# Layer 3's split row maxima and the hidden rows' clip move from VectorE to GpSimd, under a newly searched order table

## The reference, cut to what matters

```python
def _act_quant(x):
    scale = 127.0 / jnp.clip(jnp.max(jnp.abs(x), axis=-1, keepdims=True), 1e-05)
    xq = jnp.clip(jnp.round(x * scale), -128.0, 127.0) / scale
...
    gate = jax.nn.silu(_bitlinear(x, w_gate))      # 256 -> 1024
    up = _bitlinear(x, w_up)
    return _bitlinear(gate * up, w_down)           # 1024 -> 256, its input quantised too
...
    scores = jnp.einsum('bqhd,bkhd->bhqk', qh, kh)  # layer 3
    weights = jax.nn.softmax(scores, axis=-1)
```

## Time and profile before

| | |
|---|---|
| median of 3 runs | 1171.27 us (1168.84 to 1176.38) |
| the profiled execution, own time | 1171.04 us |
| its span in the trace | 1169.3 us |
| PE busy | 1042.6 us (89%) |
| DVE busy | 925.1 us (79%) |
| ACT busy | 805.6 us (69%) |
| POOL busy | 550.9 us (47%) |
| mean granted clock of PE | 0.977 |

### The profile page before, as it was taken

How to read it: one execution, slowest core, us unless ns; L and a number is a source line. 1 busy time by engine, 2 the same in 40 slices (tenths; PEclk the granted TensorE clock), 3 DMA queues, 4 the chain that set the end, 5 groups by cost and what they waited for, 6 DMA issues and landing times.

```text
span 1169.3 us, 26077 instructions
## 1 busy us (share of the span) xinstructions
PE 1042.6 (89%) x8257; PEld 776.2 (66%) x8298; DVE 925.1 (79%) x3387; ACT 805.6 (69%) x1484; POOL 550.9 (47%) x1097
## 2 busy tenths in 40 slices
PE   7989999999999988889888998888898999989986
PEld 6667778776788865766666765545566565656654
DVE  4779987878465678798986589999998999899744
ACT  5667666656665556647575667657889798899963
POOL 7232364655212456467841117756454444434343
PEclk9899999999999998989999999889999999999999
DMA  7984322325768642412358954323122222221000
GB/s 226 325 282 142 91 73 56 91 73 164 202 192 221 186 126 73 131 60 62 102 177 264 271 172 140 102 73 93 44 77 64 82 56 55 83 55 52 14 10 27
DMA packets 102326, 140.02 MB, mean 120 GB/s; under 512 B 12336, under 2 KB 79792, under 8 KB 102192
## 3 DMA queue, kind: packets, MB, share of 16 engines
q1 hardware_dynamic: 98688, 129.57, 37.8%
q0 software_dynamic: 3072, 8.39, 2.3%
q10 hardware_dynamic: 432, 0.39, 0.1%
HBM read 65.43 MB, written 22.54 MB: 75 GB/s over the span
## 4 chain that ended last, share of the span: by engine, by line
PE 39%; DVE 25%; ACT 13%; issue 7%; DMA 7%; SPq 5%; POOL 4%; DVEq 0%; another core or an unknown queue 0%; POOLq 0%; ACTq 0%
PE ps L1545 9%; PE ps L1674 4%; PE ps L1584 4%; PE ps L1566 3%; DVE ps L2239 3%; ACT probs L1996 3%; PE ps L1767 3%; PE ps L1538 3%; DVE ps L2231 3%; SPq L2862 2%; PE ps L1552 2%; DMA w<-in_expert 2%; ACT q_st L2013 2%; DVE bn L2122 2%; DVE neg_max L2243 2%
## 5 line engine op out<-in xcount | busy, mean ns | idle before, releaser
L1996 ACT ACTIVATE probs<-ps 128x384 f32<-128x384 f32 (+1 forms) x512 | 260.3, 545 | 88.8 <-PE ps L1587 52.3
L1566 PE MATMUL ps<-k_st,q_st 96*128 96x256 bf16 (+1 forms) x1024 | 173.0, 266 | 32.9 <-DVE neg_max L2231 11.8
L1584 PE MATMUL ps<-q_st,k_st 104*128 104x256 bf16 (+1 forms) x1024 | 179.5, 264 | 20.8 <-ACT probs L1996 13.0
L2013 ACT ACTIVATE q_st<-ps 8x1024 bf16<-8x1024 f32 x128 | 130.0, 1016 | 33.5 <-PE ps L1655 28.4
L1566 PEld LDWEIGHTS ps<-k_st,q_st 96*128 96x128 bf16 x1024 | 85.5, 100 | 88.9 <-DVE neg_max L2231 21.8
L2231 DVE CUSTOM_DVE_ANT_0 ps<-ps,diag_s 128x128 f32<-128x128 f32 (+1 forms) x384 | 123.4, 358 | 20.9 <-PE ps L1566 19.4
L1584 PEld LDWEIGHTS ps<-q_st,k_st 104*128 104x128 bf16 x1024 | 91.2, 99 | 66.2 <-ACT probs L1996 19.3
L2560 POOL TENSOR_SCALAR var_eps<-mv 128x2 f32<-128x2 f32 (+1 forms) x115 | 29.1, 253 | 209.9 <-DVE mv L2125 205.5
L1674 PE MATMUL ps<-probs,v 128*32 128x256 f32 (+1 forms) x2048 | 125.9, 366 | 1.7 <-ACT probs L1996 0.8
L2239 DVE CUSTOM_DVE_ANT_0 ps<-ps,mask_s 128x256 f32<-128x256 f32 x256 | 101.7, 451 | 6.8 <-PE ps L1566 6.5
L2630 POOL CAST parts<-qf 128x512 bf16<-128x512 f32 x64 | 40.1, 626 | 117.2 <-DVE qf L2152 50.6
(11 more groups left out here) (273 smaller groups left out, 2546.8 us busy)
## 6 DMA issues: line engine op xcount, KB each, us to landing
k_st<-parts SPq DMA_DIRECT2D x192, 128.0 KB
q_st<-parts SPq DMA_DIRECT2D x189, 128.0 KB
w<-in_expert SPq DMA_DIRECT2D x62, 384.0 KB, 4.3
x_rows<-wo SPq DMA_DIRECT2D x10, 768.0 KB, 10.2
ctx_t<-in_ctx_t SPq DMA_DIRECT2D x16, 256.0 KB, 3.0
ring<-x_rows SPq DMA_DIRECT2D x31, 128.0 KB, 3.4
y_rows<-ring SPq DMA_DIRECT2D x31, 128.0 KB, 3.5
xn_t<-x_rows SPq DMA_DIRECT2D x31, 128.0 KB, 4.1
```

The source lines that it names most:

```text
L1566: last = mm(t[:, c0:c0 + n], head(q_st, r, h, KROWS, j * P, P), head(k_st, r, h, KROWS, 0, n), start=j == 0 or not by_pe, stop=not by_pe, ...
L1584: last = mm(t[:, j * S:j * S + n], head(k_st, r, h, KALL, j * P, P), head(q_st, r, h, KALL, skip, n), start=j == 0 or L == 3, stop=L == 3, ...
L1996: nc.scalar.activation(probs[:, (hg % 2) * HPG + h4, 0:width], tile_of(key)[:, 0:width], ACT.Exp, scale=SCALE).then_inc(*tile_drained(key))
L2013: nc.scalar.activation(out, tile_of(key)[KROWS:KALL, 0:S].unsqueeze(1).to_broadcast([2 * HPG, HPG, S]), ACT.Copy).then_inc(*tile_drained(key))
```

## The change

Three things are changed, and the table with them.

In layer 3 (`SPLIT_BY_G = (3,)`) the two split instructions of each of the 32 groups are POOL's, in a step of their own (`split_max`) with a new lane, `max_splits`; `reduce` on DVE ends with the reduction. `turn_max` waits for the new signal `split_made` in layer 3. DVE waits for `split_made` before the first reduction of each group of the item behind a layer 3 item, since that reduction writes where POOL may still read. `hidden_clip` is the same instruction on POOL. `normalise` on DVE gets a wait for its own previous reading of `sum_inv`. Last, all tuples of `AT` are new (a search with random delays in it), and they move steps in all five queues.

```diff
-AT = (
+AT = (
...
+SPLIT_BY_G = (3,)
...
+def max_splits(part):
+    for L, b in ORDER:
+        if L in SPLIT_BY_G:
+            for hg in range(HG):
+                yield
+                part.split_max(L, b, hg)
...
-    lanes += [f(part) for f in (max_turns, max_copies, weighted_values, value_copies, value_turns, value_shares)]
+    lanes += [f(part) for f in (max_splits, max_turns, max_copies, weighted_values, value_copies, value_turns, value_shares)]
...
-                    pe.wait_ge(*max_made.at((L, b, hg)))
+                    pe.wait_ge(*(split_made if L in SPLIT_BY_G else max_made).at((L, b, hg)))
...
+                    if h4 == 0 and SLOT[L, b] and ORDER[SLOT[L, b] - 1][0] in SPLIT_BY_G:
+                        dve.wait_ge(*split_made.at((*ORDER[SLOT[L, b] - 1], hg)))
...
-                    if h4 < HPG - 1:
+                    if h4 < HPG - 1 or L in SPLIT_BY_G:
                         return
...
+                    if pair:
+                        wait_drained(dve, ("ot", L, b, pair - 1))
+                    elif SLOT[L, b]:
+                        wait_drained(dve, ("ot", *ORDER[SLOT[L, b] - 1], HG // 2 - 1))
                     V.reciprocal(sum_inv[:, :, :], t[:, :, :, DH]).then_inc(*inverted.step((L, b, pair)))
...
-                def hidden_clip(T):
-                    dve.wait_ge(*hid_round.at(T))
-                    if T >= SJ:
-                        wait_filled(dve, ("ht", T - SJ))
-                    V.tensor_scalar(hid_q[:, T % SJ, :], hid[T % SJ], ROUND, Q_MAX, ALU.subtract, ALU.min).then_inc(*hid_ready.step(T))
...
+                def split_max(L, b, hg):
+                    if hg > 1:
+                        wait_filled(pool, ("t", L, b, hg - 2))
+                    elif SLOT[L, b]:
+                        wait_filled(pool, ("t", *ORDER[SLOT[L, b] - 1], hg + 2))
+                    wait_drained(pool, ("m", L, b, hg, HPG - 1))
+                    full = neg_max[:, hg, :, :].rearrange("p h j -> p j h")
+                    hi, lo = [max_parts[:, hg % 2, :, KROWS + n * HPG:KROWS + (n + 1) * HPG] for n in range(2)]
+                    G.tensor_copy(hi, full).then_inc(*split_hi.step((L, b, hg)))
+                    pool.wait_ge(*split_hi.at((L, b, hg)))
+                    G.tensor_tensor(lo, full, hi, ALU.subtract).then_inc(*split_made.step((L, b, hg)))
+
+                def hidden_clip(T):
+                    pool.wait_ge(*hid_round.at(T))
+                    if T >= SJ:
+                        wait_filled(pool, ("ht", T - SJ))
+                    G.tensor_scalar(hid_q[:, T % SJ, :], hid[T % SJ], ROUND, Q_MAX, ALU.subtract, ALU.min).then_inc(*hid_ready.step(T))
```

More of the change, by code:

```diff
@@ L1477, in build @@
         max_hi = signal("max_hi")
+        split_made = signal("split_made")
+        split_hi = signal("split_hi")
         own_ready = signal("own_ready")
@@ L1510, in build @@
         class Idle:
-            score = exp = maxima = reduce = turn_max = rows = values = copy_output = output = normalise = k_out = lambda *_: None
+            score = exp = maxima = reduce = split_max = turn_max = rows = values = copy_output = output = normalise = k_out = lambda *_: None
             k_hi = k_rest = k_low = k_stack = q_out = q_hi = q_rest = q_low = q_stack = v_out = v_take = v_copy = ln = ln_power = lambda *_: None
```

## The result

The changed kernel takes 1191.29 us (median of 4 runs, 1181.43 to 1194.22), the kernel before 1172.01 us beside it (4 runs, 1168.84 to 1176.38). The ratio is 1.0147, 95% interval 1.0108 to 1.0185: the change made the kernel 1.5% slower, where 0.7% faster was forecast. In a later job (e14) the ratio of the same two kernels was 1.0178 (1.0133 to 1.0223). PE's mean granted clock is 0.966 in this profiled execution and 0.977 in the one of before; "What stays open" comes back to it.

A forecast was written before the change was run, and what follows sets the result against it. PE sets the pace to 700 us; from 700 to 1050 us DVE is fuller and holds PE up. The middle of -5.3 us (-11.9 + 6.6) and -12.1 us, -8.7 us, gave 1162.5 us, range 1148 to 1178.

The forecast's parts named there:

- What is put on POOL: Step pricing the moved splits and clips on POOL: 31.7 us of work, 6.6 us put back on the path.
- The term of 16 x 1.12 us: POOL's work for the sixteen hidden-row clips, each priced at 1.12 us like L2620.
- The term on the path: PE's waits for the clip in the middle stretch: three at 1.12 us each, 3.4 us.
- DVE's relief of 30.5 us: DVE busy time removed by moving 32 groups' splits (16.7 us) and 16 clips (13.8 us).
- PE's loads were to wait under 15 us for maxima: Expected profile sign, first scores' weight loads from 700 to 1050 us: under 15 us where they waited 24.1.
- The splits' price: Cost of layer 3's two split instructions on POOL: 0.22 + 0.21 us, 0.50 us a pair with the wait between.
- rival (4): At `turn_max` in PE's queue: POOL's in-order queue delivers splits late, +13.7 us, 1185 us; chance 0.12.
- Rival (2): The new table frees PE's idle time in the first 700 us, 10.7 us more, 1152 us; chance 0.13.
- Rival (3): The read port shared by DVE and POOL takes the relief back: -2.3 us, 1169 us; chance 0.15.
- the forecast's -8.7 us: Whole-kernel gain, the middle of a count by the chain (-5.3 us) and one by DVE's queue (12.1 us).
- 12.1 us of the loads' waits for maxima: Count by DVE's queue: half of PE's 24.1 us of weight-load waits for row maxima vanishes.
- the 12.2 steps for 8.5 of the turns: New table's PE steps between a layer 3 group's last `maxima` and its turn, covering a POOL late by two or three.

The follow-up runs named there:

- e14: The changed kernel measured once more, unaltered, against the kernel before in a later job: 1.0178, 1182.00 us beside 1165.14.
- e8: Kernel before plus sixteen POOL instruction forms behind the last store, timed singly: on 1024 values mult with add 1.05 us, subtract with min 3.65.
- e5: Changed kernel with POOL's clip written as mult by 1.0 and add -ROUND, without the limit to 127: 0.9919 of the kernel before, 1162.38 us.
- e1: Changed kernel with layer 3's splits and the clip back on DVE, so only the new table remains: 1.0021 of the kernel before, 1167.05 us.
- e7: Kernel before with its old table, only layer 3's splits moved to POOL: 1.0012 of the kernel before.
- e9: Kernel before with its old table, only the clip moved to POOL, in the mult-and-add form: 0.9994 of the kernel before.
- e10: Kernel before with its old table, layer 3's splits and the mult-and-add clip both on POOL: 1.0066 of the kernel before.
- e15: Changed kernel with the mult-and-add clip on POOL, measured again in a later job: 0.9933 of the kernel before, 1156.76 us beside 1165.14.
- e2: Changed kernel with only the clip back on DVE; layer 3's splits stay on POOL, new table: 0.9961 of the kernel before, 1159.03 us.
- e6: Changed kernel with POOL's clip as a single subtraction of ROUND, no second operation: 1.0019 of the kernel before.
- e16: Changed kernel with the clip on DVE and six useless subtract-with-min instructions at its POOL place, not waiting for DVE's clip: 1.0163 of the kernel before.

## Why the prediction was wrong

**The step that failed** is in "What is put on POOL": "The clip has the length and kind of L2620: 1.12 us." It has the length, not the kind. L2620 multiplies and adds; the clip subtracts and takes a minimum, and that is 3.65 us on POOL (e8). The term of 16 x 1.12 us was 16 x 3.7 us. The term on the path fell with it: three waits of 1.12 us, 3.4 us, were seven waits and 14.6 us in the same stretch, and 34.6 us of clips on the chain; in e5, with the short clip, PE's waits for it are 0.8 us. No bound was drawn for the clip's length, which was the second fault: a price was taken from the nearest row by size, as if the operations made no difference.

The trace of before did hold a warning, in rows that the prediction doesn't use. These are POOL's instructions of the routing; L2706 is add with mult, L2741 mult alone, both on 16 elements, and L2743 add with max on 32:

```profile
L2706 POOL TENSOR_SCALAR nblk<-cnt x8: 202/203/203, 149.9 to 572.0; 128x16 f32<-128x16 f32 x8
...
L2741 POOL TENSOR_SCALAR less<-nblk x8: 269/274/281, 154.7 to 576.8; 128x16 f32<-128x16 f32 x8
...
L2743 POOL TENSOR_SCALAR past<-past x8: 327/333/337, 155.4 to 577.5; 128x32 f32<-128x32 f32 x8
```

One operation takes 71 ns more than two on the same 16 elements. And if 0.2 us of L2743 are the start, some 0.1 us remain for 32 elements, over 3 ns each, which scaled to 1024 would have given 3 to 4 us instead of 1.12.

**The other terms.** DVE's relief of 30.5 us was 34.8 by the busy times, or 27.2 against the new table with the old work (e1). PE's loads were to wait under 15 us for maxima in the middle stretch and waited 18.6. The splits' price was right, and the place of rival (4) was not the trouble: PE waited for POOL's splits once in the changed kernel, for 0.7 us. Its mechanism, an in-order queue on POOL that comes late, has a part in the loss all the same, behind the clip: three of the ten pieces on the chain, 8.4 us. Rival (2) fell with e1: the table alone is 1.0021, and the first 700 us were unchanged. Rival (3), the port: with a clip of about the assumed length the change does pay, so the port doesn't take the whole relief back. The Trainium skill's warning (page "Perfetto Trace Analysis", section "Optimizing Scalar/DVE Operations") that offloading between these two might not help holds for e7, e9 and e10 in its outcome, and not for e5 and e15.

**The sum with the right clip.** Where the clip takes the 1.12 us of the forecast, as in e5 and e15, the kernel stands at 0.9919 and 0.9933 of before; the forecast's -8.7 us of 1171.04 are 0.9926. So the sum was close with that term in the place of the other. That it was close for its reasons is not shown, and may be luck. The sum let 12.1 us of the loads' waits for maxima vanish. From 620 us to the end these waits are 28.0 us before and 21.8 in e5, 6 us less. In e10, with the same moves under the old table, they are 22.4, and the kernel is at 1.0066: the relief alone doesn't give the gain.

**By the length of the clip,** splits on POOL and the new table throughout:

| the clip | mean us of one | ratio |
|---|---|---|
| on DVE (e2) | 0.75 | 0.9961 |
| on POOL, mult and add (e5, e15) | 1.12 | 0.9919, 0.9933 |
| on POOL, subtract (e6) | 2.86 | 1.0019 |
| on POOL, subtract and min (changed, e14) | 3.70 | 1.0147, 1.0178 |

From 1.12 to 3.70 us are 2.58 x 16 = 41 us on POOL, and they cost (0.0147 - (-0.0081)) x 1172 = 27 us by the first pair, which is from two jobs, and 1182.00 - 1156.76 = 25 us by e14 and e15, side by side in one. So somewhat under two thirds of it came through.

**What stays open.** How the slow clip's loss divides between late rows and a held queue isn't measured: the case of late rows with a free queue wasn't tried. The chain of the changed kernel gives the larger part to the late rows, 26.2 us against 8.4, and e16 shows only that a somewhat longer hold is enough by itself.

A part of the loss shows as PE's own busy time. With the same 8298 matmuls on record, PE is busy for 1048.9 us at a mean granted clock of 0.974 in e14 and 1038.5 us at 0.984 in e15, 10 of the 25 us between the two, and all of it behind 620 us. Whether the lower clock only follows from PE's longer waits isn't shown; the two kernels differ in nothing but the clip's form, so it is brought about by that form in one way or another.

Nor is it settled why the moves pay under the new table and not under the old one (old: splits 1.0012, clip 0.9994, both 1.0066; new, from 1.0021: splits 0.9961, clip 1.0001, both 0.9919 and 0.9933). The ratios with both moves are from different chips. What the traces show is that POOL's answers come in better time under the new table: with both moves PE waits for the clip and the splits 6.1 + 3.0 us under the old table (e10), and 0.8 + 1.5 or 2.2 + 1.8 us under the new one (e5, e15). That is 5 to 7 us of the 15 to 17 that lie between the ratios. It agrees with the 12.2 steps for 8.5 of the turns, and doesn't prove that they are the reason.

The best version is e5: the change with the clip as `1.0, -ROUND, ALU.mult, ALU.add`, which leaves out the limit to 127.

## What to carry to other kernels

When an instruction is moved to GpSimd, take its price from a row of the same operations, not only of the same size; where there is none, bound it from the slowest row for each element, or time it by itself behind the last store, which took one run here. An engine that is busy half of the time can still be late: 2.6 us more at 16 places cost 25 to 27 us, mostly where PE waited for the result, and in part where the queue's next steps stood behind it. And a change that is written together with a new order is best measured apart, the order alone and each move alone, since here a loss of 2 to 3% hid a gain of 0.7 to 0.8%.

## What the runs showed of the hardware

- GpSimd's two-operation instruction with immediates takes 1.05 us on 128x1024 f32 for mult with add, and 3.65 us for subtract with min, add with max, add with min and mult with min; a single subtract or min takes 2.78 us, longer than mult and add together. The Trainium skill, page "GPSIMD Engine Reference", section "Engine selection", has it that work with one input runs at roughly line rate on GpSimd. The page has no figure for a form. If mult with add and the cast (1.05 and 1.04 us) are taken as that rate, the other forms are 2.6 to 3.5 times slower; the measurement decides.
- The type of the output, bf16 or f32, made no difference to any of the three forms that were timed with both.
- Moving the 32 pairs and 16 clips took 27.2 us of busy time off DVE (917.5 us in e1, 890.3 in the changed kernel, under one table), where their undisturbed time was 21.9 us: stalls like those of the earlier trace rows went with them.
